# Summing gathered tiles with the one-hots as weights on four column strips, in a two-layer graph kernel

## What is computed

```
h = relu(layernorm(x))
msg = where(type == 0, h[src] @ W_data.T + b_data, h[src] @ W_control.T + b_control)
x = x + relu(segment_sum(msg, dst) + h @ W_self.T + b_self)                # layer 0
h = relu(layernorm(x));  deg = max(number of edges into a node, 1)
e = (tanh(p_dst[dst] + p_src[src] + b) + tanh(yn)) * 0.5 * d[dst] * d[src]  # d = deg ** -0.5
x = x + segment_sum(h[src] * e, dst)                                       # layer 1
```

## Time and profile before

| | before |
|---|---|
| median of three runs | 7954.81 us (7938.12 to 7955.42) |
| profiled execution | 7983.53 us, span 7981.7 us |
| TensorE matmuls (PE) busy | 5574.0 us, 70% of the span |
| TensorE weight loads (PEld) | 4349.5 us, 54% |
| VectorE (DVE) | 4589.0 us, 57% |
| ScalarE (ACT) | 2870.7 us, 36% |
| GpSimd (POOL) | 4367.9 us, 55% |
| mean granted TensorE clock | 0.745 of full speed |

### The profile page before, as it was taken

The page is one execution under the profiler, slowest core; times in us unless marked ns, Lnnn a source line. Parts: engine busy times, 40 slices in busy tenths (PEclk is TensorE's granted clock), DMA queues, the critical chain, the costliest instruction groups (busy, mean ns, idle before and its releaser), DMA issues. The chain is left out here.

```text
span 7981.7 us, 117499 instructions
## 1 busy us (share of the span) xinstructions
PE 5574.0 (70%) x28538; PEld 4349.5 (54%) x28538; DVE 4589.0 (57%) x16809; ACT 2870.7 (36%) x9992; POOL 4367.9 (55%) x4284
## 2 busy tenths in 40 slices
PE   5677777777777777777775566777776777777663
PEld 4555555555555555555554545565655565555553
DVE  5755555555555555555444556666666666666662
ACT  4433333333333333333332333333433333333330
POOL 5644444444444444444455366666766666666654
PEclk7577777777777776777776767777878778877875
DMA  6644444444444444444455434444444444444433
GB/s 196 199 139 130 132 135 130 135 135 132 132 136 131 132 136 130 131 131 134 128 165 161 121 85 97 103 100 98 104 98 101 102 103 100 102 101 101 101 90 91
DMA packets 764976, 979.74 MB, mean 123 GB/s; under 512 B 135667, under 2 KB 567063, under 8 KB 763799
## 3 DMA queue, kind: packets, MB, share of 16 engines
q1 hardware_dynamic: 620131, 687.26, 30.0%
q0 software_dynamic: 135168, 281.42, 14.3%
q10 hardware_dynamic: 9012, 3.56, 0.2%
HBM read 911.05 MB, written 60.67 MB: 122 GB/s over the span
## 5 line engine op out<-in xcount | busy, mean ns | idle before, releaser
L564 POOL DMA_INDIRECT G<-t,IDX x4016 | 4077.9, 1015 | 3263.9 <-PE PS L874 1578.9
L699 ACT ACTIVATE OHF<-PS 128x384 bf16<-128x384 f32 x1764 | 853.8, 490 | 2522.5 <-PE PS L892 1313.0
L1031 PE MATMUL PS<-HTB,OWF 128*128 128x129 f32 x3528 | 945.8, 359 | 839.7 <-ACT HTB L801 341.4
L1031 PEld LDWEIGHTS PS<-HTB,OWF 128*128 128x128 f32 x3528 | 813.8, 252 | 1165.9 <-issue 743.1
L782 ACT ACTIVATE ST<-PS,MV 128x1 f32<-128x1 f32 x1764 | 460.1, 261 | 1953.4 <-issue 1670.1
L904 PE MATMUL PS<-CDST,OHF 128*128 128x256 bf16 x5292 | 1115.9, 331 | 7.6 <-issue 5.8
L1040 PE MATMUL PS<-CDST,HTB 128*128 128x256 f32 x2352 | 926.3, 485 | 0.0
L868 PEld LDWEIGHTS PS<-OHF,G 128*128 128x128 f32 x4224 | 814.3, 295 | 154.6 <-issue 108.8
L868 PE MATMUL PS<-OHF,G 128*128 128x32 f32 x4224 | 800.4, 360 | 134.6 <-DVE ACC L1549 52.5
L904 PEld LDWEIGHTS PS<-CDST,OHF 128*128 128x128 bf16 x5292 | 633.2, 120 | 458.6 <-issue 249.0
L1247 DVE TENSOR_SCALAR CDST<-IO,BASE 128x256 bf16<-128x256 int16 x1764 | 503.1, 296 | 590.0 <-PE PS L904 301.2
(11 more groups left out here) (229 smaller groups left out, 8072.4 us busy)
## 6 DMA issues: line engine op xcount, KB each, us to landing
HTB<-t0s SPq DMA_DIRECT2D x442, 384.0 KB
OWF<-t0s SPq DMA_DIRECT2D x440, 384.0 KB
HTB<-t SPq DMA_DIRECT2D x882, 132.0 KB
G<-t,IDX POOLq DMA_INDIRECT x4016
YN<-rows SPq DMA_DIRECT2D x882, 64.0 KB
OHF<-rows SPq DMA_DIRECT2D x882, 64.0 KB
t0s<-HTB SPq DMA_DIRECT2D x25, 384.0 KB
t0s<-OWF SPq DMA_DIRECT2D x24, 384.0 KB
```

The source lines that it names most:

```text
L564: eng.indirect_dma_start(out=G[:, k:k + width], out_offset=None, in_=table, in_offset=bass.IndirectOffsetOnAxis(ap=at, axis=0)).then_inc(s ...
L699: eng.activation(X0[:, k % KX, :, :].rearrange("p n w -> p (n w)"), PS[:, cell_bank(k), 0:384], ACT.Identity).then_inc(q_ev, 1)
L1031: eng.matmul(cell_slot(k), OT1[c % RT][:, col:col + 128], TC1[c % RT][:, k % HB, 0:D + 1], start=True, stop=True).then_inc(d_ga, 1)
```

## The change

In the steps (not in the last part of 104 tiles) the roles of the two operands are swapped. The one-hot of a tile (32 columns) is now the weights, and the gathered tile (128 columns) is streamed. The eight products go to four groups of 32 partitions of the bank: tile c * 2 + h to strip c, so that a strip holds the sum of two tiles, nodes on partitions and features along the free axis. That is the wrong way round for ACC, and there are two partial sums per quad. So ScalarE copies the 128 x 128 block out of PSUM (`strips_out`, `strips_out1`), and TensorE makes one f32 product with that block as weights and the matrix SEL (128 x 64, ones where a strip's row belongs to a quad's column) streamed. This adds the two halves of each quad and turns the block (`sums_into`). Only then does VectorE add to ACC: it waits for `r_sum` in place of `m_pe` or `e_pe`.

Where the new instructions stand: ScalarE's copy of step s - 1 is the first thing in its loop of step s, ahead of the first cell. TensorE's product for step s - 1 comes after the first cell of step s and ahead of the second, behind a wait for the copy (`r_so`). GpSimd's wait for the slot is the same as before. SEL is made once by VectorE. The code table's turn moves to other columns of the bank, and some semaphores are shared.

```diff
+        SEL = IOTA[:, 64:128]
...
+        STRIPS = [YN[:, HTE:HTE + D], OWF[:, 1792:1792 + D]]
...
             eng.wait_ge(q_ga, NG * NB)
+            eng.wait_ge(r_sum, SM)
             eng.dma_start(YN[:, 0:T], ew).then_inc(q_ew, 16)
...
+            def strips_out(s):
+                eng.wait_ge(m_pe, s + 1)
+                if s >= 1:
+                    eng.wait_ge(r_sum, s)
+                eng.activation(STRIPS[0], PS[:, s % 2, 0:D], ACT.Identity).then_inc(r_so, 1)
...
                     if UNIT[s] + i < UNIT[s + 1]:
                         unit_parts(UNIT[s] + i)
+                    if i == 0 and s >= 1:
+                        strips_out(s - 1)
                     if CELL[s] + i < CELL[s + 1]:
                         evacuate(CELL[s] + i)
...
+            def strips_out1(s):
+                eng.wait_ge(e_pe, s + 1)
+                eng.wait_ge(r_sum, SM + s)
+                eng.activation(STRIPS[1], PS[:, s % 2, 0:D], ACT.Identity).then_inc(r_so, 1)
...
                     k = CELL1[s] + i
+                    if i == 0 and s >= 1:
+                        strips_out1(s - 1)
                     if k < CELL1[s + 1]:
                         cell1(k)
...
+            def strips_into(s, hots, width):
+                for h in range(2):
+                    for c in range(4):
+                        j = c * 2 + h
+                        k = (s % S * TG + j) * width
+                        ins = eng.matmul(PS[c * W:(c + 1) * W, s % 2, 0:D], hots[:, j, :], G[:, k:k + D],
+                                         start=h == 0, stop=h == 1)
+                return ins
...
+            def sums_into(n, s):
+                return eng.matmul(PS[:, s % 2, D:D + 2 * W], STRIPS[n], SEL, start=True, stop=True).then_inc(r_sum, 1)
...
             for s in range(SM):
-                for i in range(max(CELL[s + 1] - CELL[s], TILE[s + 1] - TILE[s])):
+                for i in range(max(CELL[s + 1] - CELL[s], TILE[s + 1] - TILE[s], 2)):
                     k, t = CELL[s] + i, TILE[s] + i
+                    if i == 1 and s >= 1:
+                        eng.wait_ge(r_so, s)
+                        sums_into(0, s - 1)
                     if k < CELL[s + 1]:
                         gather(k)
...
                 eng.wait_ge(m_g[s % S], main_full(0, s))
-                tiles_into(0, s % 2, s, OH[:, s % 2 * 2, :, :])
-                degrees_into(s % 2, OHS[:, s % 2 * 2:s % 2 * 2 + 1 + CNTS[s + 1] - CNTS[s], :, :]).then_inc(m_pe, 1)
+                strips_into(s, OH[:, s % 2 * 2, :, :], D)
+                degrees_into(s % 2, OHS[:, s % 2 * 2:s % 2 * 2 + 1 + CNTS[s + 1] - CNTS[s], :, :],
+                             D + 2 * W).then_inc(m_pe, 1)
...
                 for k in range(CELL1[s], CELL1[s + 1]):
+                    if k == CELL1[s] + 1 and s >= 1:
+                        eng.wait_ge(r_so, SM + s)
+                        sums_into(1, s - 1)
                     gather1(k)
...
                 eng.wait_ge(m_g[s % S], main_full(1, s))
-                tiles_into(1, s % 2, s, OW[:, s % 2, :, :]).then_inc(e_pe, 1)
+                strips_into(s, OW[:, s % 2, :, :], W1).then_inc(e_pe, 1)
...
+            halves = IDENT[:, :].rearrange("p (q h w) -> p q h w", h=2, w=W)
+            eng.tensor_tensor(SEL.rearrange("p (q w) -> p q w", w=W), halves[:, :, 0, :], halves[:, :, 1, :],
+                              ALU.add).then_inc(s_k, 1)
...
             def item_add(s, v, t, n, q, zadds):
                 at = quad(t // QT + q, v)
-                eng.wait_ge(m_pe, s + 1)
+                eng.wait_ge(r_sum, s + 1)
...
             def adds1(s, zadds):
-                eng.wait_ge(e_pe, s + 1)
+                eng.wait_ge(r_sum, SM + s + 1)
```

More of the change, by code:

```diff
@@ L273, in gnn_program @@
         b_t, b_x1, b_hd, b_t2, b_pd = sems("b_t", "b_x1", "b_hd", "b_t2", "b_pd")
-        c_x, c_s = a_x[0:5], [sem(f"c_s{n}") for n in range(3)]
+        c_x, c_s = a_x[0:5], a_x[5:8]
         c_t, c_o = sems("c_t", "c_o")
@@ L278, in gnn_program @@
         m_pe, m_oh, m_os, m_ib = sems("m_pe", "m_oh", "m_os", "m_ib")
+        r_so, r_sum = sems("r_so", "r_sum")
         q_b, q_p, q_tri, q_rk, q_r, q_tab, q_te, q_dec = sems(
@@ L507, in _ @@
             for c in range(NC - 3, NC):
-                eng.wait_ge(c_s[c % 3], landed(c, 3))
+                eng.wait_ge(c_s[c % 3], 2 * landed(5 + c % 3) + landed(c, 3))
         @block.gpsimd
@@ L736, in _ @@
                     rows_out(ROWS.index(s))
+            strips_out(SM - 1)
             eng.wait_ge(q_ap, NG * NB)
@@ L818, in _ @@
                         eng.activation(TH[:, s % 2, :], SS[:, s % 2, :], ACT.Tanh).then_inc(e_th, 1)
+            strips_out1(SM - 1)
             for k in (NG * NB, NG * NB + 1):
@@ L870, in tiles_into, with degrees_into @@
                 return ins
-            def degrees_into(bank, hots):
+            def strips_into(s, hots, width):
[6 more added lines that the diff above has]
+                return ins
+            def degrees_into(bank, hots, at=2 * W):
                 width = 2 * W * hots.shape[1]
-                return eng.matmul(PS[:, bank, 2 * W:2 * W + width], TRI[:, 1, :],
+                return eng.matmul(PS[:, bank, at:at + width], TRI[:, 1, :],
                                   hots.rearrange("p a q w -> p (a q w)"), start=True, stop=True)
@@ L955, in _ @@
                     eng.matmul(PS[:, 6, 0:NG + 2], ONES[:, :], FLG[:, :], start=True, stop=True).then_inc(s_f0, 1)
+            eng.wait_ge(r_so, SM)
+            sums_into(0, SM - 1)
             for k in range(NG * NB - LATE, NG * NB):
@@ L1051, in _ @@
                 eng.wait_ge(m_g[s % S], main_full(1, s))
-                tiles_into(1, s % 2, s, OW[:, s % 2, :, :]).then_inc(e_pe, 1)
+                strips_into(s, OW[:, s % 2, :, :], W1).then_inc(e_pe, 1)
+            eng.wait_ge(r_so, 2 * SM)
+            sums_into(1, SM - 1)
             for k in range(NG * NB - LATE1, NG * NB):
@@ L1325, in code_rows @@
             def code_rows(g):
-                got = PS[0:NB, TURN[g] % 2, 256:384]
+                got = PS[0:NB, TURN[g] % 2, 384:512]
                 eng.wait_ge(q_tr, g + 1)
+                eng.wait_ge(r_sum, TURN[g] + 1)
                 if g >= 2:
@@ L1779, in _ @@
                 if c >= 3:
-                    eng.wait_ge(c_s[c % 3], landed(c - 3, 3))
+                    eng.wait_ge(c_s[c % 3], 2 * landed(5 + c % 3) + landed(c - 3, 3))
                 for i in range(CB):
```

13 lines of the change are left out of this document (8 added, 5 removed).

## The result

The changed kernel takes **7598.29 us** (median of four runs, 7570.72 to 7627.19) against 7950.7 before (four runs): ratio 0.956, 95% interval 0.9518 to 0.9601. The forecast was 7800 with a range of 7640 to 8200. The direction was right; the gain of 350 us is more than twice the 155 forecast, and the time lies just outside the range, beside the rival "all four strips at once" (7635).

The account below looks back on a forecast made before the run. PE's signals arrive late while POOL gathers, so layer 0 pays for late sums and layer 1 sits on POOL's floor. 206 x (1.2 - 0.5) = 144, plus 5 and 10, is 159 us less: 7824, scaled and rounded 7800; range 7640 to 8200.

Parts of the forecast that it names:

- all four strips at once: Rival: strips work side by side, run 1.3 us, 290 us won in layer 0, 30 in layer 1; 7635 us, chance 0.13.
- The ring of layer 0: Layer 0's 17.3 us step: POOL waits for PE's sums, which follow cells delayed until POOL's gathers release late signals.
- the floor of layer 1: About 12.1 us per step, eight gathers and the release; layer 1 (12.6 us) sits on it.
- The run on the strips: PE's 16 sum passes: 2.05 us in place of 3.46 at 1.2 GHz, 1.2 us less per step of layer 0.
- lower bound of 1.3: Shortest run foreseen: four strips side by side, four streams (0.85) behind 32-column loads (0.86, partly beside them), about 1.3 us.
- What a us of run is worth: In layer 0 each us at the sums' products is a us of the step; in layer 1 nearly none.
- The turn: PE's added product with SEL and ACT's copy, layer 0: 0.5 us per step, bounds 0 to one cell of 1.25.
- it also adds one signal to those that come late: Part of the turn's price in layer 0: one more PE signal among the late ones; no separate size given.
- DVE's adds: Their wait for r_sum costs nothing; if that signal is late, 0.8 us moves behind the release, covered by the 1.25 bound.
- Layer 1: PE stands before its second cell for ACT's copy: cost 0; some of 24 long POOL waits (189 us) go, 10 us won.
- 1.4 us of slack: Layer 1: the run of sums ends at 9.4 to 10.4 us after POOL's start, ahead of the release at 11.8.
- the slip of that rival: Layer 1's chain ends after the release; half of 249 steps lose 3.5 us (435 us): 8240 us, chance 0.18.

Follow-up runs that it names:

- e7: Changed kernel with half of the gathers (four per step after the first five steps of a layer), late-signal chip: 5430.73 us, 0.6891 of the kernel before.
- e8: Kernel before with two of the eight products of a step's sums, late-signal chip: 7497.9 us, ratio 0.9519.
- e1: Changed kernel with layer 1 as before (old products, no copy or turn there), on a chip with prompt signals (kind P): 5843.21 us, ratio 0.9967.
- e4: Changed kernel with the products taken strip by strip (two loops swapped), prompt-signal chip: 5841.8 us, ratio 0.9963 to the kernel before.
- e5: Kernel before, unchanged, run again for its trace on a second late-signal chip: 7881.87 us, ratio 0.9994.
- e6: Changed kernel, unchanged, run again on the second late-signal chip: 7480.51 us, ratio 0.9488 to the kernel before.
- e16: Kernel before with layer 0's turn and wait added and its sums made the old way, late-signal chip: 7943.65 us, ratio 1.0109.
- e9: Changed kernel with one PE signal for two products at three places (applies and placed tiles), late-signal chip: 7504.23 us, 0.9524 of the kernel before.
- e11: Kernel before plus only ACT's copy in layer 1 and PE's wait for it ahead of its second cell, late-signal chip: 7737.68 us, ratio 0.9811.
- e10: Changed kernel with layer 0's sums moved ahead of the step's last one or two cells, late-signal chip: 7402.41 us, 0.9402 of the kernel before.
- e15: Changed kernel with layer 0's sums moved ahead of the step's last three or four cells, prompt-signal chip: 6031.51 us, 1.0267 of the kernel before.

## Why the prediction was off, point by point

- **What bounds the kernel: right.** The ring of layer 0 and the floor of layer 1 hold (12.13 us against "about 12.1"); e7 and e8 bear out both halves. One word is too wide: PE's signals are late only from some gathers into POOL's run on, not during all eight. That the lateness belongs to the chip, and not to the kernel's order, chips P add: the same code (e1) shows no pause and 10.3 us per step.
- **The run on the strips: the term that failed.** "PE starts products in order, so only one tile's second pass runs beside the next tile's first" gave 2.05 us. It is 1.08 at 1.2 GHz, since PE starts passes of different strips ahead of the program's order, four at a time (e4): four rounds of 0.213 us and the rest of the last stream. That is under the lower bound of 1.3 too, because the 32-column loads are hidden: those of the second four start 1506.94 to 1506.96, while the first four streams run (1506.91 to 1507.35). Mean 0.94, so 2.15 us are saved per step in place of 1.2. The Trainium skill ("TensorE: Matmul & The Clock Gate", The mechanism) says in one place that a load overlaps only where the row group differs, which would have made the strips worthless; the trace is against it. The same page's 2.38x (Measured speedup vs the span model, three strips, one pass) is in line with the 3.35 of four strips and two passes here.
- **What a us of run is worth: taken too high.** The text took 1.0. Between steps 36 and 240 the step fell by 1.38 us (3494 to 3213 us in 204 steps) for 2.15 of run and the turn. With the turn at 0.1 to 0.3 a us of run is worth 0.7 to 0.8, as in e8 (0.8). By the text's own rule with the true run, 206 x (2.15 - 0.5) = 340; the trace has 300. A part of the 1.38 may not be the run's at all, but the clock's: from before to after the granted clock of layer 0 rose from 0.73 to 0.80, and from e5 to e6 PE's other products (without run and turn, 500 to 3600 us) fell from 9.6 to 9.0 us a step. The text had no term for that, and no run tells how much of it reaches the step. e8's clock rose too (0.79).
- **The turn: 0.5 forecast, 0.1 to 0.3 measured (e16).** The bounds (0 to 1.25) held. For the part "it also adds one signal to those that come late" e9 gives no support. DVE's adds cost nothing, as forecast: no wait of DVE for the turn is among its larger ones.
- **Layer 1: the second term that failed.** The text had PE's stand at the second cell, its place and its partners right, and priced it as a cost with 1.4 us of slack, and a gain of 10. The slack held, so the slip of that rival did not come. But of the long waits, which it knew to follow an early `e_pe`, it took only 10 us as won, without a reason. PE's stand removed nearly all of them: 118 us in the profiled execution, 145 in e11.
- **The sum.** 300 + 118 - 5 = 413 where 144 + 5 + 10 = 159 stood. Of the 254 us missing, 151 are layer 0's, 108 layer 1's. The part between the layers takes 5 back. The medians' gain is smaller, 352 us. On the chip of e5 and e6 the profiled executions are 383 us apart, 265 in layer 0 and 110 in layer 1.
- **The range.** It left half of the fastest case out, by intent. Two favourable sizes came together, the fastest strips and a gain in layer 1, for which even the fastest rival had only 30 us. That rival, all four strips at once, was right in how the strips work. Its 290 us for layer 0, against 300 measured, are luck in part: the run came out shorter than its 1.3 us and the turn cheaper than its 0.5, while a us of run was worth less than its 1.0.

## What to carry to other kernels

Small products on disjoint column strips run at the same time even if each strip gets two passes in a row: price them by the longest strip, not by the sum or by an order of starts, and price what this saves at the wait that ends last (here 0.8 us per us in layer 0, none in layer 1). Where a consumer's release comes late and in bulk, a wait added at a place that stands idle anyway can gain time by keeping the steps in one rhythm; look at the step before each long one, not only at the long one. The rhythm is the reading that fits the traces; that the wait gains the time is measured. Such gains depend on the chip: 4 to 5% for the whole change where PE's signals come late, 0.4% where POOL alone sets the step (e4, which differs from the changed kernel only in the order of the strips; that kernel itself wasn't run there). Moving the sums one or two cells up brings some 1% more on the first kind (e10); on the second it wasn't measured, and three or four cells up (e15) lose 2.7% there.

## What the runs showed of the hardware

- The same program took 7872 us on one chip and 5861 on another. In the one, PE's signals are prompt (0.04 us to ACT's start) outside POOL's run of indirect DMAs and in its first gather or two, and up to 6.6 us late from there on (kernel before; 7.2 in after). In the other ACT resumes within 0.06 us of a product's end all the time, while POOL gathers without a pause (e4). What differs between the chips stays open. The runs tell only that the time goes with the gathers (e7) and doesn't fall with fewer signals (e9).
- Passes on different strips of 32 columns start within 20 ns of each other in fours, and within 45 ns even where the program puts four passes of one strip first (e4). On one strip they start 0.213 us apart at 1.2 GHz.
- Sixteen f32 streams of 128 columns on four strips take 1.08 us at 1.2 GHz and 0.64 at 2.4; on one strip 3.62 and 1.93. The one-strip run is 0.2 us over 16 x 0.213. That is the last stream's own record (0.42 us long), so no cost of going in and out of the strips is seen.
